# A third raw slot in the ring of adjacency loads, and five instead of six slots for the weight tiles

## The reference, cut to what matters

```
def _L0_gnn_ref(z, dist_matrix, W, B):            # CUTOFF = 1, MU = 1, SIGMA = 0.5
    msg = z @ W + B
    sens = exp(-(1.0 / dist_matrix - 1.0 / MU) ** 2 / (2.0 * SIGMA * SIGMA))
    weights = where(dist_matrix < CUTOFF, sens, 0.0)
    return weights @ msg

def _L1_gnn_ref(x, adj, W):
    A_hat = adj + eye(adj.shape[0])
    d_inv_sqrt = sum(A_hat, axis=1) ** (-0.5)
    A_norm = d_inv_sqrt[:, None] * A_hat * d_inv_sqrt[None, :]
    return relu(A_norm @ (x @ W.T))

h = maximum(_layernorm(x), 0.0)
x = x + _L0_gnn_ref(h, adj, L0_gnn_W, L0_gnn_B)
h = maximum(_layernorm(x), 0.0)
x = x + _L1_gnn_ref(h, adj, L1_gnn_W)
```

## Time and profile before

| | |
|---|---|
| median of 3 runs | 627.53 us (626.89 to 627.85) |
| profiled execution | 632.89 us, of which 631.1 us are its span |
| PE busy | 537.5 us, 85% of the span |
| DVE busy | 485.1 us, 77% |
| ACT busy | 466.0 us, 74% |
| mean granted TensorE clock | 0.949 of full speed |
| DMA | 145.14 MB, 230 GB/s over the span |

### The profile page before, as it was taken

How to read it: one execution, slowest core, us unless ns; L and a number is a source line. 1 busy time by engine, 2 the same in 40 slices (tenths; PEclk the granted TensorE clock), 3 DMA queues, 4 the chain that set the end, 5 groups by cost and what they waited for, 6 DMA issues and landing times.

```text
span 631.1 us, 4420 instructions
## 1 busy us (share of the span) xinstructions
PE 537.5 (85%) x1509; PEld 243.6 (39%) x1509; DVE 485.1 (77%) x555; ACT 466.0 (74%) x306; POOL 39.6 (6%) x68
## 2 busy tenths in 40 slices
PE   2446896969877998779769999979999999999995
PEld 2133432323322443334324444434444444444442
DVE  2799977789759899989989979986799849202056
ACT  2286878789967969999999969992999777920010
POOL 0241500000000000000000000000000000101100
PEclk9997998879888999989979999979999999999998
DMA  7999999999999959999999999999699951295623
GB/s 151 197 277 272 277 335 278 277 265 245 313 300 265 202 102 303 307 233 188 306 304 201 203 212 282 270 266 197 236 224 219 233 126 67 93 376 226 236 60 75
DMA packets 87193, 145.14 MB, mean 230 GB/s; under 512 B 4225, under 2 KB 78210, under 8 KB 78210
## 3 DMA queue, kind: packets, MB, share of 16 engines
q1 hardware_dynamic: 82130, 108.15, 75.2%
q0 software_dynamic: 5040, 36.70, 16.2%
HBM read 106.04 MB, written 38.80 MB: 230 GB/s over the span
## 4 chain that ended last, share of the span: by engine, by line
PE 42%; DVE 21%; ACT 14%; DMA 12%; issue 7%; SPq 4%; DVEq 0%
PE acc L377 13%; DMA raw<-in_adj_dram 12%; PE mix L399 11%; PE mix L390 11%; DVE kept L648 9%; DVE wt L663 4%; ACT wt L528 3%; ACT wt L533 3%; ACT wt L538 3%; SPq L281 3%; ACT wt L547 3%; DVE wt L669 2%; DVE rowpart L656 2%; PE acc L399 2%; PE side L399 1%
## 5 line engine op out<-in xcount | busy, mean ns | idle before, releaser
L377 PE MATMUL acc<-wt,msg 128*128 128x512 f32 x512 | 242.0, 617 | 4.7 <-ACT wt L547 4.7
L648 DVE STREAM_TRANSPOSE kept<-raw 128x2048 f32<-128x2048 f32 x64 | 147.6, 2306 | 42.9 <-DMA raw<-in_adj_dram 31.4
L377 PEld LDWEIGHTS acc<-wt,msg 128*128 128x128 f32 x512 | 98.6, 199 | 134.1 <-issue 124.3
L528 ACT ACTIVATE wt<-wt 128x2048 f32<-128x2048 f32 x64 | 121.9, 1905 | 38.1 <-DVE wt L663 38.1
L663 DVE SCALAR_TENSOR_TENSOR wt<-kept 128x2048 f32<-128x2048 f32 x64 | 146.5, 2288 | 1.5
L533 ACT ACTIVATE wt<-wt 128x2048 f32<-128x2048 f32 x64 | 121.6, 1900 | 0.4
L390 PE MATMUL mix<-kept,support 128*128 128x512 f32 x224 | 106.2, 620 | 13.0 <-DVE kept L648 6.5
L547 ACT ACTIVATE wt<-wt 128x2048 f32<-128x2048 f32 x52 | 98.8, 1899 | 0.0
L538 ACT ACTIVATE wt<-wt 128x2048 f32<-128x2048 f32 x52 | 98.7, 1898 | 0.0
L399 PE MATMUL mix<-late,support 128*128 128x512 f32 x200 | 89.7, 592 | 0.0
L656 DVE TENSOR_REDUCE rowpart<-raw 128x16 f32<-128x4096 f32 x20 | 87.6, 4379 | 0.0
(11 more groups left out here) (87 smaller groups left out, 260.8 us busy)
## 6 DMA issues: line engine op xcount, KB each, us to landing
raw<-in_adj_dram SPq DMA_DIRECT2D x128, 512.0 KB, 12.5
adj_t_spill<-kept SPq DMA_DIRECT2D x35, 1024.0 KB, 13.4
late<-adj_t_spill POOLq DMA_DIRECT2D x27, 1024.0 KB, 10.9
raw<-adj_t_spill POOLq DMA_DIRECT2D x8, 1024.0 KB, 6.2
x<-in_x_dram SPq DMA_DIRECT2D x32, 64.0 KB, 7.5
out_dram<-kept SPq DMA_DIRECT2D x32, 64.0 KB, 1.8
w_sb<-in_L_gnn_W_dram SPq DMA_DIRECT2D x1, 64.0 KB
late<-in_L_gnn_W_dram SPq DMA_DIRECT2D x1, 64.0 KB
```

What stands on the lines that cost most here:

```text
L377: mm = nc.tensor.matmul(acc0[:], msg[:, col(u) * T + k, :], wt[:, u % WTS, k, :], start=(first and k == 0), stop=(last and k == T - 1))
L528: nc.scalar.activation(v, v, ACT.Ln, bias=LN_GUARD).then_inc(ln_done, 1)
L648: nc.vector.transpose(dst, src).then_inc(turned, 1)
```

## The change

The constants give `raw` three slots and `wt` five. In bytes of each partition a slot of `raw` is 16 KB and one of `wt` 8 KB. SP issues the load of pair 2 before its loop, so that behind odd unit u it now issues the load of pair u // 2 + 3. In the tail there are six halves of `raw` slots instead of four, and POOL's wait for the last pair that used a slot is worked out by n % RAW.

```
-RAW, KEPT, WTS, LATE = 2, 4, 6, 3
+RAW, KEPT, WTS, LATE = 3, 4, 5, 3
@@ sync, before the loop
             load_x(2)
             load_x(3)
+            load(2)
             for u in range(UNITS):
                 if spills(u):
                     sp.wait_ge(turned, u + 1)
                     store(u)
                 if u % 2 == 1 and u // 2 + RAW < PAIRS:
                     load(u // 2 + RAW)
@@ gpsimd, late loads
                 elif slot >= LATE:
-                    last_pair = PAIRS - RAW + (slot - LATE) // 2
+                    last_pair = max(n for n in range(PAIRS) if n % RAW == (slot - LATE) // 2)
                     pool.wait_ge(summed, last_pair + 1 - PE_SUMS * C4)
                     pool.wait_ge(turned, 2 * last_pair + 2)
```

## The result

| | before | after |
|---|---|---|
| median | 627.68 us (626.89 to 630.83, 5 runs) | 621.72 us (618.51 to 624.14, 5 runs) |
| profiled execution | 632.89 us, span 631.1 | 618.51 us, span 616.7 |

The ratio is 0.9896, with a 95% interval of 0.9859 to 0.9933. Run twice more beside the experiments, the same kernel gave 0.9867 (0.9825 to 0.9909) and 0.9887 (0.9843 to 0.9930). The change makes the kernel faster by 1.0 to 1.3%, 6.5 to 8.4 us. The forecast was 620.9 us, 6.6 us faster. The ratios leave out single executions that took over 1.5% longer than the fastest of their kernel.

What follows compares the result with a forecast made beforehand. DMA was taken to bound the kernel up to unit 20's transpose, DVE from 218 to 325 us, then PE and ACT in turn. Gains of 2.8 + 3.8 = 6.6 us gave 627.5 - 6.6 = 620.9 us, range 614.5 to 627.5.

Steps and rivals of the forecast that it cites:

- What bounds the kernel: Whole span: DMA limits up to unit 20's transpose, DVE from 218 to 325 us, then PE and ACT in turn.
- The first stretch: Up to unit 20's transpose: one store less ahead, 2.8 us gained, the wait for `raw` turning into one for `spilled`.
- the time is used up by bytes: Ahead of unit 20's transpose: queued pairs, stores and loads back sum to 183.6 us, 185.6 with the start.
- The third rival: First stretch: a third load in flight raises the rate and 25.7 us of waits go; 598.0 us in all, chance 0.08.
- At unit 18 the gain is nil: First stretch, unit 18: nothing gained from the new load order, since unit 15 is not stored.
- The load at the start: Before SP's loop: four more DMAs ahead of the first store cost 0; without cover up to 10.4 us.
- The second stretch: Past 216 us: pair 14 fills the DMA hole and the waits for pairs 16 and 19 go, 3.8 us.
- Does PE follow?: At unit 38: PE starts 6.6 us earlier, its idling shrinks to 3.0 us, and ACT follows in full.
- Five slots: Ring of `wt`: `cut` waits for PE, worst 7.4 us at unit 52, under a wait already there; cost 0.
- The second rival: Groups 5 to 7: the ring of `wt` becomes the limit, costing 15.2 or 22.8 us; 636.1 us with 15.2; chance 0.12.
- The clock: PE at unit 38: with shorter idling perhaps 2.6 us more come back, giving 618.3 us; kept only in the range.
- The sum: Whole kernel: 2.8, 1.9 and 1.9 us gained, 6.6 us off the median of 627.5, giving 620.9 us.

Runs made afterwards that it cites:

- half a place less: Changed kernel with SP issuing the load of pair u // 2 + 2 between a pair's two stores; 0.9906 of the kernel before.
- late only: Changed kernel with loads one pair further ahead only from pair 13 on, old queue order up to pair 12; 0.9947 of the kernel before.

## Why the prediction was right, point by point

- **What bounds the kernel.** Right in the main. The experiments with parts of the change add, and two or three loads back taken from ahead of unit 20 moved its transpose by 4.5 to 7.7 us. One load back less, with six wt slots, moved nothing.
- **The first stretch, 2.8 us.** The wait did turn from `raw` into `spilled`, as predicted, and did not go. By time it gained 4.2 us (2.3 to 6.1), which holds 2.8; the traces say more, 5.5 us at unit 20. Bytes ahead of it account for half: from 2 us to its start 47.6 MB moved in the changed kernel and 48.8 MB before, about one store less. The step that failed is "the time is used up by bytes", at one price for pairs and one for stores. From 40 to 175 us its prices are too high by 5% already before the change, by 8 to 9% in three traces with the new order and by 6% in the fourth; and the 377 GB/s come from a window of 5 us in which 0.5 of 1.9 MB were pairs. That the sum gave 185.6 us for 184.8 is in part luck: it counts 47.2 MB, where 48.8 MB had moved by then. The DMA share was 1.06 to 1.08 in all seven traces, so that it didn't show that more could be had. What made the mixed traffic cheaper stays open: the depth of the queue is the obvious candidate, but the same depth ran at 283 GB/s with six wt slots, and half a place less ran at 293 GB/s up to 150 us. The third rival, given 0.08, is refuted for pairs by themselves (198 GB/s), and its 25.7 us were far too large. "At unit 18 the gain is nil" was wrong too: it was 3.3 us.
- **The load at the start, 0.** Right: unit 4's transpose starts at 53.99 us instead of 54.28, and has no wait.
- **The second stretch, 3.8 us.** Right: 3.3 us by time (1.7 to 5.0). The hole is nearly filled, and the waits at units 32 to 40 are gone.
- **Does PE follow?** Only in part as worked out. PE's wait before unit 38 shrank to 0.19 us, not to 3.0, for ACT's copy, on which PE's work before it hangs, came 6.9 us earlier and not 3.6, once more of the first stretch was gained. ACT lost its slack instead: its wait at the copy of group 5 is 1.08 us, where it was 5.81. More than about 1 us from DVE's side would probably have been lost on ACT; no run shows it.
- **Five slots, 0.** Right, with its mechanism: the wait at unit 52 stands where it was predicted, 5.79 us with `make_x1` 1.51 us behind, and the ring costs nothing that can be measured (1.0002, within 2 us). The second rival, given 0.12, describes the ring of four: it was one slot away.
- **The clock, left out.** Open. The 2.45 us at unit 38 show in the changed kernel's trace. With two raw and five wt slots PE has no long wait there either (0.29 us, and 3.70 us for the eight products). But the kernel before with two loads held, which has two raw and six wt slots, does have it:

```profile
320.44 5.93 PE L392 MATMUL mix<-kept,support 128*128 128x512 f32 x8 [5.86 <-DVE kept L650]
```

  So it is more than an accident of one trace, and two traces don't tell how often it falls in the kernel before. The interval of the measured gain (4.2 to 8.9 us) is too wide to show these 2.45 us.
- **The sum.** 2.8 + 3.8 = 6.6 us were forecast; 4.2 + 3.3 = 7.5 by parts, 6.5 to 8.4 in all. The mechanism holds in the second stretch and for the ring of five. In the first it gives half of what the traces show, and that the total fits so well (6.5 us against 6.6 in the first comparison) is in part luck.

## What to carry to other kernels

A ring's extra slot in a stretch that a DMA queue limits is worth about what no longer stands ahead of the awaited transfer, not the waits that it seems to remove: write out the order of the queue for one consumer and count the bytes. Take the count as a first size only (here 2.8 us counted, 5.5 seen and 25.7 of waits), and check its prices on a stretch of mixed traffic, not only on the whole sum. Follow the count on to the next waiting consumer, too, before calling bytes moved away a gain. When a ring is made smaller, reading each new wait against the slack behind it works as long as every one is covered; with one slot less the loss was 24 us where 0 to 4 had been read off, so the smallest margin is what counts. And read a rate from every trace of a kind: three here have 291 to 294 GB/s, and the fourth has 283.

## What the runs showed of the hardware that I had not expected

- The DMA share doesn't tell the rate. It is 1.14 at 198 GB/s with pairs alone (late only, 220 to 235 us) and 1.04 at 381 GB/s where 3.3 of 3.8 MB are stores and loads back (the change's last trace, 165 to 175 us). A share above 1 does not mean that no more can be had.
- Mixed loads and stores moved 5 to 9% faster than the rates read from two short windows would have it. The rule of the Trainium skill that I had weighed and set aside (page "DMA: Bandwidth & Descriptors", section "Specifications", line rate from 512 B on and a ceiling of 435 GB/s) is not borne out for the pairs: in rows of 1 KB and without a hole they stayed at 198 to 201 GB/s with two slots and with three.
- Single executions of one kernel spread by more than 1%: the kernel before from 624.74 to 635.23 us over 33 runs. One trace of each kernel gave 14.4 us for a change that is worth 6.5 to 8.4.
